# A GRU cell feeding a Runge-Kutta integrator on one core: VectorE's and GpSimd's work of a time step in another order

## What is computed

```python
# GRU cell, h0 = cond
gi = x_t @ W_ih + b_ih;  gh = h @ W_hh + b_hh      # 3 x 512 columns: r, z, n
r, z = sigmoid(i_r + h_r), sigmoid(i_z + h_z)
n = tanh(i_n + r * h_n)
h = (1 - z) * n + z * h
x1_t = x_t + h

# integrator, q0 = p0 = cond, DT = 0.01
def derivative(q, p, drive):
    dq = q - q**3 / 3 - p + drive + tanh(q) @ coupling.T + bias
    dp = 0.08 * (q + 0.7 - 0.8 * p)
    return dq, dp
# dq1..dq4 at (q, p), (+ DT/2), (+ DT/2), (+ DT);  drive = x1_t
q = clip(q + DT/6 * (dq1 + 2*dq2 + 2*dq3 + dq4), -20, 20);  p likewise
out_t = x1_t + q
```

## Time and profile before

| | us |
|---|---|
| median of 3 runs | 1072.88 (1070.92 to 1073.58) |
| the profiled execution's own time | 1072.05 |
| its span, first to last instruction | 1070.0 |
| busy: TensorE matmul / weight load | 949.5 / 930.4 |
| busy: VectorE | 962.5 |
| busy: ScalarE / GpSimd | 570.6 / 281.1 |

### The profile page before, as it was taken

The page is one execution under the profiler, slowest core; times in us unless marked ns, Lnnn a source line. Parts: engine busy times, 40 slices in busy tenths (PEclk is TensorE's granted clock), DMA queues, the critical chain, the costliest instruction groups (busy, mean ns, idle before and its releaser), DMA issues.

```text
span 1070.0 us, 54115 instructions
## 1 busy us (share of the span) xinstructions
PE 949.5 (89%) x23809; PEld 930.4 (87%) x23809; DVE 962.5 (90%) x2352; ACT 570.6 (53%) x1485; POOL 281.1 (26%) x390
## 2 busy tenths in 40 slices
PE   6689999999999999999999999999999999997674
PEld 6689999988998998998998899899899889997664
DVE  5669999999999999999999999999999999999987
ACT  5545555555555555555555555555555555554442
POOL 2112222222222222222222222222222222222221
PEclk9799999999999999999999999999999999999997
DMA  9001011010100101101010010100100100000000
GB/s 344 12 8 32 23 33 28 25 31 28 33 23 28 32 23 33 28 23 32 28 30 25 28 33 23 33 28 23 33 28 30 31 13 23 23 18 18 23 13 11
DMA packets 29321, 35.71 MB, mean 33 GB/s; under 512 B 3616, under 2 KB 27936, under 8 KB 28960
## 3 DMA queue, kind: packets, MB, share of 16 engines
q1 hardware_dynamic: 29088, 32.27, 9.4%
HBM read 23.87 MB, written 8.39 MB: 30 GB/s over the span
## 4 chain that ended last, share of the span: by engine, by line
DVE 67%; issue 18%; ACT 8%; PE 4%; DMA 1%; DVEq 1%; SPq 0%; POOL 0%; POOLq 0%; ACTq 0%
DVE q L544 9%; DVE y L547 7%; DVE ps_own L674 7%; DVE ps_own L544 6%; DVE th_lo L544 6%; DVE base L547 5%; DVE y_sum L544 5%; DVE ps_rk L544 3%; DVE q_raw L544 3%; ACT ps_act L447 3%; ACT th_hi L451 3%; DVE b_raw L544 2%; DVE cube L674 2%; DVE h_lo L544 2%; DVE z_part L564 2%
## 5 line engine op out<-in xcount | busy, mean ns | idle before, releaser
L279 PE MATMUL ps_rk<-th_hi,cpl_lo 128*128 128x64 f16 x4096 | 163.9, 194 | 97.4 <-ACT th_hi L451 95.6
L279 PEld LDWEIGHTS ps_rk<-th_hi,cpl_lo 128*128 128x128 f16 x4096 | 136.8, 98 | 115.6 <-issue 109.9
L319 PE MATMUL ps_gi<-xs_hi,wih_hi 128*128 128x256 f32 x728 | 215.9, 297 | 2.0 <-ACT gi L409 1.9
L319 PE MATMUL ps_gi<-xs_lo,wih_hi 128*128 128x256 f32 x728 | 206.1, 283 | 0.0
L319 PE MATMUL ps_gi<-xs_hi,wih_lo 128*128 128x256 f32 x728 | 205.7, 283 | 0.0
L447 ACT ACTIVATE ps_act<-q 128x256 f32<-128x256 f32 x256 | 98.1, 383 | 174.7 <-DVE q L544 161.6
L279 PE MATMUL ps_rk<-th_lo,cpl_hi 128*128 128x64 f16 x4096 | 163.5, 194 | 0.0
L279 PE MATMUL ps_rk<-th_hi,cpl_hi 128*128 128x64 f16 x4096 | 163.0, 194 | 0.0
L319 PEld LDWEIGHTS ps_gi<-xs_hi,wih_hi 128*128 128x128 f32 x728 | 139.5, 192 | 2.4 <-ACT gi L409 2.4
L544 DVE SCALAR_TENSOR_TENSOR th_lo<-ps_act,th_hi 128x256 f16<-128x256 f32 x256 | 107.4, 420 | 36.2 <-ACT ps_act L455 35.9
L319 PEld LDWEIGHTS ps_gi<-xs_lo,wih_hi 128*128 128x128 f32 x728 | 139.7, 192 | 0.0
(11 more groups left out here) (143 smaller groups left out, 1964.9 us busy)
## 6 DMA issues: line engine op xcount, KB each, us to landing
ring<-x_in SPq DMA_DIRECT2D x64, 128.0 KB, 2.4
out<-ring SPq DMA_DIRECT2D x64, 128.0 KB, 2.1
xs_raw<-x_in SPq DMA_DIRECT2D x60, 128.0 KB, 2.1
gi<-wih_in SPq DMA_DIRECT2D x4, 768.0 KB, 7.1
whh_raw<-whh_in SPq DMA_DIRECT2D x4, 768.0 KB, 9.8
cpl_raw<-cpl_in SPq DMA_DIRECT2D x1, 1024.0 KB, 14.8
q<-cond_in SPq DMA_DIRECT2D x1, 128.0 KB, 6.7
h<-cond_in SPq DMA_DIRECT2D x1, 128.0 KB, 6.7
```

Of the source, the lines that this page charges most:

```text
L279: mm = nc.tensor.matmul(ps[:, m * B:(m + 1) * B], w[:, k, w_cols + m * P:w_cols + (m + 1) * P], v[:, k * B:(k + 1) * B], start=False, stop ...
L319: last = nc.tensor.matmul(ps[:, 0:CHUNK * B].rearrange("p (j b) -> p j b", j=CHUNK), w[:, k, m * P:(m + 1) * P], v[:, :, k, :], start=(r = ...
```

## The change

y and b_mid share one PSUM tile, `y_b`, updated in place. The weighted sum of the three y and the kept b is built by one instruction a stage (`sum_b`) in place of two `end_y_sum` on VectorE and `total_y` on GpSimd; `end_b` adds q's share. e1 is computed unscaled (`e1_raw`, with an immediate scalar), and ScalarE scales it twice, into PSUM (`seed_e1`) and into SBUF (`scale_e1`). The drive goes to GpSimd, unscaled. The seed comes directly behind y, and b_mid just ahead of q; `cell_n_in` and `cell_h` go behind the q of their stage. On ScalarE `gate_rz` goes to the next step's first stage, `gate_n` behind the second square, `split_h_hi` behind the third, `keep_b` to the end of the step before. `gates_rz` waits for h_lo only ahead of its third part. On GpSimd the order is output sum, q_step, h_minus_n, x1, xs_lo, drive. The diff, without the declarations and setup constants:

```diff
@@ -294,8 +291,9 @@
                     pe.wait_ge(rz_seeded, u + 1)
-                    pe.wait_ge(h_lo_ready, u + 1)
-                product(ps_rz, 2 * K, whh_hi, whh_lo, 0, h_hi, h_lo, rz_summed, first, end)
+                    pe.wait_ge(h_hi_ready, u + 1)
+                product(ps_rz, 2 * K, whh_hi, whh_lo, 0, h_hi, h_lo, rz_summed, first, end,
+                        before_lo=lambda: pe.wait_ge(h_lo_ready, u + 1))
@@ -435,8 +433,12 @@
             def seed_e1(u):
-                act.wait_ge(e1_ready, u + 1)
-                nc.scalar.activation(ps_rk[0][:, 0:KB], e1[:, :], ACT.Copy).then_inc(e1_seeded, 1)
+                act.wait_ge(e1_raw_ready, u + 1)
+                nc.scalar.activation(ps_rk[0][:, 0:KB], e1_raw[:, :], ACT.Copy, scale=rk_scale[:, 0:1]).then_inc(e1_seeded, 1)
+            def scale_e1(u):
+                act.wait_ge(e1_raw_ready, u + 1)
+                nc.scalar.activation(e1[:, :], e1_raw[:, :], ACT.Copy, scale=rk_scale[:, 0:1]).then_inc(e1_ready, 1)
@@ -494,6 +496,8 @@
             seed_e1(0)
+            scale_e1(0)
+            keep_b(0)
@@ -503,25 +507,24 @@
                 square(t, 0)
-                keep_b(t)
-                if t == 0:
-                    gate_rz(1)
+                if more_cells:
+                    gate_rz(t + 1)
                 if more_gates:
                     seed_rz(t + 2)
-                if more_cells:
-                    gate_n(t + 1)
                 tanh(t, 1)
...
                 square(t, 1)
+                if more_cells:
+                    gate_n(t + 1)
+                if more_pieces:
+                    store_gi(first)
                 if more_gates:
                     seed_n(t + 2)
-                if more_pieces:
-                    store_gi(first)
-                if more_cells:
-                    split_h_hi(t + 1)
                 tanh(t, 2)
...
                 square(t, 2)
+                if more_cells:
+                    split_h_hi(t + 1)
                 if splits_x(t):
@@ -531,10 +534,10 @@
                     store_gi(first + 2)
-                if more_gates:
-                    gate_rz(t + 2)
-                if more_cells:
+                if more_cells:
+                    keep_b(t + 1)
                     seed_e1(t + 1)
+                    scale_e1(t + 1)
             for t in range(T):
...
@@ -671,6 +666,9 @@
                 dve.wait_ge(sq_ready, 4 * t + s + 1)
+                if s == 1:
+                    dve.wait_ge(n_in_ready, min(t + 2, T))
                 nc.vector.scalar_tensor_tensor(out=cube[:, :] if s == 0 else part, in0=sq, scalar=-OWN[s], in1=q[:, s, :],
@@ -698,49 +696,57 @@
             def stage_y(t, s):
                 wait(dve, q_ready, 4 * t + s)
...
                     wait(dve, b_ready, t)
-                    tt(y[:, 0, :], q[:, 0, :], b_state[:, :], ALU.subtract, y_ready)
+                    wait(dve, b_raw_ready, t)
+                    tt(y_b, q[:, 0, :], b_state[:, :], ALU.subtract, y_ready)
                 else:
                     dve.wait_ge(b_mid_ready, 2 * t + s)
-                    tt(y[:, s, :], q[:, s, :], b_mid, ALU.subtract, y_ready)
+                    tt(y_b, q[:, s, :], y_b, ALU.subtract, y_ready)
...
-                dve.wait_ge(y_ready, 3 * t + s + 1)
-                fma(b_mid, y[:, s, :], B_STEP, b_state[:, :], b_mid_ready)
+                dve.wait_ge(e_seeded, 3 * t + s + 1)
+                dve.wait_ge(b_sum_ready, 3 * t + s + 1)
+                fma(y_b, y_b, B_STEP, b_state[:, :], b_mid_ready)
...
                 dve.wait_ge(y_ready, 3 * t + s)
-                fma(ps_rk[s % 2][:, 0:KB], y[:, s - 1, :], minus_y[:, s - 1:s], e1[:, :], e_seeded)
+                dve.wait_ge(e1_ready, t + 1)
+                fma(ps_rk[s % 2][:, 0:KB], y_b, minus_y[:, s - 1:s], e1[:, :], e_seeded)
...
                 wait(dve, b_ready, u)
-                fma(e1[:, :], b_state[:, :], minus_b[:, 0:1], drive[:, :], e1_ready)
+                fma(e1_raw[:, :], b_state[:, :], -1.0 / BETA, drive[:, :], e1_raw_ready)
+            def sum_b(t, s):
+                dve.wait_ge(y_ready, 3 * t + s + 1)
+                if s == 0:
+                    dve.wait_ge(b_kept_ready, t + 1)
+                    fma(b_sum[:, 0, :], y_b, B_STEP / 3, b_kept[:, :], b_sum_ready)
+                elif s == 1:
+                    dve.wait_ge(b_sum_ready, 3 * t + 1)
+                    fma(b_sum[:, 1, :], y_b, 2.0 * B_STEP / 3, b_sum[:, 0, :], b_sum_ready)
+                else:
+                    dve.wait_ge(b_sum_ready, 3 * t + 2)
+                    dve.wait_ge(e_seeded, 3 * t + 3)
+                    fma(y_b, y_b, (2.0 - 2.0 * B_STEP) * B_STEP / 3, b_sum[:, 1, :], b_sum_ready)
...
-            def end_y_sum(t, i):
-                if i == 0:
-                    dve.wait_ge(y_ready, 3 * t + 2)
-                    fma(y_sum[:, 0, :], y[:, 1, :], 2.0, y[:, 0, :], y_sum_ready)
-                else:
-                    dve.wait_ge(y_ready, 3 * t + 3)
-                    dve.wait_ge(y_sum_ready, 2 * t + 1)
-                    fma(y_sum[:, 1, :], y[:, 2, :], 2.0 - 2.0 * B_STEP, y_sum[:, 0, :], y_sum_ready)
             def end_b(t):
-                dve.wait_ge(y_total_ready, t + 1)
-                dve.wait_ge(b_kept_ready, t + 1)
-                fma(b_raw[:, :], y_total[:, :], B_STEP / 3, b_kept[:, :], b_raw_ready)
+                dve.wait_ge(b_sum_ready, 3 * t + 3)
+                dve.wait_ge(q_ready, 4 * t + 3)
+                fma(b_raw[:, :], q[:, 3, :], B_STEP / 3, y_b, b_raw_ready)
@@ -754,53 +760,52 @@
             split_h_lo(0)
-            dve.wait_ge(cpl_scaling, 14)
-            cell_drive(0)
             start_e(0)
...
                 stage_y(t, 0)
-                stage_b(t, 0)
                 seed_e(t, 1)
+                sum_b(t, 0)
                 split_tanh_lo(t, 0)
...
                     cell_n_rh(t + 1)
+                stage_b(t, 0)
+                stage_q(t, 0)
+                if more_cells:
                     cell_n_in(t + 1)
-                stage_q(t, 0)
                 stage_y(t, 1)
-                stage_b(t, 1)
                 seed_e(t, 2)
...
                 stage_cube(t, 1)
+                sum_b(t, 1)
                 stage_base(t, 1)
...
                     cell_z(t + 1)
+                stage_b(t, 1)
+                stage_q(t, 1)
+                if more_cells:
                     cell_h(t + 1)
-                stage_q(t, 1)
                 stage_y(t, 2)
-                if more_cells:
-                    split_h_lo(t + 1)
                 seed_e(t, 3)
...
                 stage_cube(t, 2)
+                sum_b(t, 2)
                 stage_base(t, 2)
-                end_y_sum(t, 0)
-                end_y_sum(t, 1)
+                if more_cells:
+                    split_h_lo(t + 1)
                 stage_q(t, 2)
...
                 end_q_sum(t)
-                if more_cells:
-                    cell_drive(t + 1)
+                end_b(t)
                 split_tanh_lo(t, 3)
                 stage_cube(t, 3)
+                clip_b(t)
                 stage_base(t, 3)
-                end_b(t)
-                clip_b(t)
                 if more_cells:
@@ -835,6 +840,11 @@
+            def cell_drive(u):
+                pool.wait_ge(x1_ready, u + 1)
+                add(drive[:, :].rearrange("p (k b) -> p k b", b=B), ring[:, u % SLOTS, :].rearrange("p (k b) -> p k b", b=B),
+                    rk_bias[:, :].unsqueeze(2).broadcast_to([P, K, B]), drive_ready)
             def add_out(t):
@@ -842,11 +852,6 @@
                 subtract(q_step[:, :], q[:, 1, :], q[:, 0, :], q_step_ready)
-            def total_y(t):
-                pool.wait_ge(y_sum_ready, 2 * t + 2)
-                pool.wait_ge(q_ready, 4 * t + 3)
-                add(y_total[:, :], y_sum[:, 1, :], q[:, 3, :], y_total_ready)
@@ -859,24 +864,23 @@
             cell_x1(0)
+            pool.wait_ge(consts_ready, 1)
+            cell_drive(0)
...
                 if t >= 1:
-                    pool.wait_ge(e_seeded, 3 * t + 1)
+                    pool.wait_ge(y_ready, 3 * t + 1)
                     add_out(t - 1)
+                step_q(t)
                 if more_cells:
                     cell_d(t + 1)
-                pool.wait_ge(e_seeded, 3 * t + 2)
-                step_q(t)
+                    cell_x1(t + 1)
                 if splits_x(t):
-                    pool.wait_ge(rk_summed, 4 * t + 2)
+                    pool.wait_ge(h_lo_ready, t + 3)
                     split_x_lo(t + AHEAD)
-                pool.wait_ge(e_seeded, 3 * t + 3)
-                if more_cells:
-                    cell_x1(t + 1)
-                pool.wait_ge(sq_ready, 4 * t + 4)
-                total_y(t)
+                if more_cells:
+                    cell_drive(t + 1)
             for t in range(T):
```

More of the change, by code:

```diff
@@ L84, in gru_rk4_kernel @@
         rk_bias = sb("rk_bias", [P, K])
-        drive_bias = sb("drive_bias", [P, K])
         n_bias = sb("n_bias", [P, KB])
```

(19 more changed lines are left out.)

## The result

| | before | after |
|---|---|---|
| median, us | 1071.9 (4 runs, 1069.05 to 1073.58) | 978.97 (4 runs, 976.71 to 980.08) |
| ratio | | 0.913, 95% interval 0.9105 to 0.9161 |
| the profiled execution's own time / its span, us | 1072.05 / 1070.0 | 979.96 / 977.5 |
| a step with projections, clip to clip, us | 15.74 | 14.28 |
| the six steps without projections, us | 15.2 to 16.0, the last 14.8 | 13.8 to 13.9, two of 15.2 and 15.3, the last 13.2 |

The change makes the kernel 8.7% faster. The forecast was 987 us with a range of 979 to 1010, so the time lies a hair under the range: direction and mechanism as forecast, the size 8 us short.

What follows compares the result with a forecast made beforehand. VectorE was taken as the bound before, TensorE after in steps 1 to 57. Span 1070.0 - 74.8 (steps 1 to 53) - 10.4 (54 to 63) - 0.7 (step 0, setup) = 984.1, plus 2.05 and 0.8: 987 us, range 979 to 1010.

Steps and rivals of the forecast that it cites:

- VectorE's chain by itself: VectorE's summed instruction spacings over one step, clip to clip: 13.87 us, 0.45 under what TensorE needs.
- The holds on b_mid and on the first y_sum: Two VectorE instructions reading two SBUF tensors, lengthened over GpSimd instructions: 0.25 + 0.50 = 0.75 us a step, to go.
- the new one on q_sum: Stage 4: q_sum falls on GpSimd's xs_lo and ends some 0.36 us late, with nothing lost.
- A dependent neighbour: On VectorE, an instruction needing its predecessor's result costs 0.11 us more than an independent one.
- The second rival: VectorE's order gives nothing and only the holds go: 0.75 us a step, 47 us less, 1026 us; chance 0.04.
- scale_e1, the drive's add and the later xs_lo: Work added or moved on ScalarE and GpSimd: forecast to cost nothing in a TensorE-bound step.
- the floor of 14.35 us a step: Steps 1 to 57: TensorE's block lengths, 14.32 us, plus 0.03 for starts not quite back to back.
- Step 0 and the setup: Step 0 gains 1.3 us behind its q1 and 0.2 ahead, less 0.8 for added setup work: 0.7 saved.
- Steps 58 to 63: Last six steps, without projections, bound by VectorE: 5 x 13.95 + 13.0 + 3.6 = 86.4 us.
- price for the lower clock: Last six steps: 3.6 us added because TensorE, partly idle, runs part of the time at 1.2 GHz.
- From the span to the median: Added to the 984.1 us span: 2.05 for the profiled execution's own time, 0.8 for the median of runs.
- the rivals on the slow side: VectorE still bound 1007 us (0.15), only holds go 1026 (0.04), GpSimd holds 1104 (0.03), blocked queue 1015 to 1050 (0.06).

## Why the prediction was right or wrong

Right, by its own steps:

- The bound moves from VectorE to TensorE: chain, window and the pair of kernels with fewer projections (956.8 us after, no change before).
- VectorE's chain by itself: 13.87 us forecast, 13.82 measured with fewer projections, each stage within 0.06.
- The holds on b_mid and on the first y_sum go, and the new one on q_sum is hidden.
- A dependent neighbour costs about 0.11 us and an independent one nothing: order alone gave 0.49 us a step, at most 0.13 of it by shorter holds. This decides between the trace and the rule of the Trainium skill, "VectorE: DVE Perf Modes", section "The DRAIN you can't avoid", by which the order could not matter; the measurement is the other way. The second rival left out that this section of the Trainium skill goes on: "A next op that is not held starts earlier". The trace agrees with that sentence: independent neighbours are 0.32 to 0.34 us apart.
- scale_e1, the drive's add and the later xs_lo cost nothing in steps 1 to 57.

Wrong: the size, 987.0 against 979.0 us. The span was forecast as 984.1 and is 977.5. The step that failed most is the floor of 14.35 us a step put down for TensorE, which measured 14.28; three smaller terms erred the same way, and the four make the 8 us.

- TensorE's floor, 3.9 us. The step put 14.32 into the sum and added 0.03 "for starts that are not quite back to back"; the step is 14.28. 57 x 0.07 = 4 us (888.66 - 74.65 = 814.0 us for steps 1 to 57, forecast 818). The 14.32 took 2.14 for the first 72 gate matmuls, a distance from before with a small gap in it: the last eight matmuls of the block start at 969.78, 0.27 us ahead of the coupling, and in after at 515.03, 0.23 ahead of it. Without the gap the block is 2.10, as the other 72. The added 0.03 had no row behind it.
- Step 0 and the setup, 1.5 us. The clip after step 0 was forecast at 76.2 and came at 74.65. I gave step 0 a steady, TensorE-bound rest; it runs on VectorE's chain, 10.9 us from q1 to the clip where 11.4 were counted. The other 1.0 lies ahead of its q1. There the sum added 0.8 us for scale_e1 and keep_b, but n_rh waits for TensorE's gate products, 6.23 us at 63.10 in after, and that wait covers both; q1 came 0.4 us earlier than before. Part may be scatter: over the kernels run here that keep th_lo, whose setups are nearly the same, that clip came anywhere from 74.1 to 78.5 us.
- Steps 58 to 63, 1.2 us: 85.2 against 86.4. No row of the prediction shows its price for the lower clock, 3.6 us. In after two of the steps take 15.2 and 15.3 us at a granted clock of 0.89, beside 13.8 to 13.9 at 1.00, so the price was 2.8. The steps at full clock are 0.1 shorter than the 13.95 counted, and the last is 0.2 longer, 13.2.
- From the span to the median, 1.4 us: 2.05 over the span and 0.8 more were added by the executions of before; here the own time is 2.46 over the span, and the median of four is 0.99 below it.

The last matmuls of the 2.14 in the kernel before, followed by the coupling at 970.05 of the earlier trace rows:

```profile
969.78 0.40 PE L279 MATMUL ps_rz<-h_lo,whh_hi 128*128 128x64 f16 x8
```

The range was at fault more than the forecast. Its lower end stood 8 us below the forecast while 57 steps hung on one sum of block lengths: 0.04 us of reading in it is 2.3 us, and setup and executions scatter by some 3 us each. An end 12 us below would have been the honest one. The chance went to the rivals on the slow side, none of which came, and too little was left for a floor read too high.

What stays open: what lowers the clock in some of the last steps and not in others. In after they are the first and the fourth of the six; with one extra instruction the first and the last two, and with the drive's add on VectorE only the last, 16.3 us at 0.58. TensorE's idle share alone doesn't tell them apart: the steps at 1.00 have it too, 10.2 us of work in 13.8.

## What to carry to other kernels

When one engine's dependent chain bounds a loop, sum the other engines' gapless block lengths before pricing the change: they say where the gain will stop, and here they gave it to 0.3%. For such a floor take the shortest distance at which a block of its shape was seen, multiply the error of reading by the number of repetitions, and put it into the lower end of the range. An order is worth as much as the pairs it separates, until the next engine's queue is full; from then on it buys slack (0.46 us a step here), and slack is what lets the drive's add, a hold of 0.2 to 0.36 us and an extra scaling pass for nothing.
